# Two sparse graph-attention layers on one Trainium2 core: a distance mask for owners, fewer small copies in the first phase, and an earlier write of the second table

## The chip, the cores and the metric

The kernel runs on one core of one Trainium2 chip. The metric is device time in microseconds: the median of 3 timed runs before the change is 1710.78 us (1709.91 to 1712.45). The profile is one further execution of 1709.7 us, of which the traced span is 1708.0 us.

## The reference

Both layers work on 8192 nodes with 128 features. The adjacency matrix is dense int32, 8192 x 8192 (268 MB), but holds only about nine ones in a row.

```python
h = jnp.maximum(_layernorm(x, axis=-1), 0.0)
x = x + _L0_gnn_ref(h, adj, W, a)
h = jnp.maximum(_layernorm(x, axis=-1), 0.0)
x = x + _L1_gnn_ref(h, adj, Wq, bq, Wk, bk, Wv, bv)

# layer 0                                    # layer 1
h = x @ W                                    q, k, v = x @ Wq.T + bq, x @ Wk.T + bk, x @ Wv.T + bv
e = leaky_relu(s1[:, None] + s2[None, :])    scores = q @ k.T / sqrt(d)
scores = where(adj > 0, e, -9e15)            scores = where(adj > 0, scores, -9e15)
attention = softmax(scores, axis=1)          attention = softmax(scores, axis=-1)
out = elu(attention @ h)                     out = elu(attention @ v)
```

## The kernel before, in words

Work goes by tiles of 128 rows, 64 of them, each phase in groups of four. The first phase (the functions called `survey`, one on each engine) reads the adjacency matrix once, turns each row into a list of at most 24 neighbours, and does layer 0. The second phase (`attend`) uses the kept lists and does layer 1; it does not read the matrix again.

One step `t` of the first phase works on several tiles at once:

- SyncE (SP) loads the matrix in quarters of a tile (128 x 2048 int32, 1 MB, line 455) into two tile buffers. A load waits until ScalarE has turned the quarter that lay there into a mask (`mask_done`). In the same in-order queue stand the load of a tile's own rows of the first table (line 468), and once in four steps the write of four finished tiles to the second table (line 489).
- ScalarE (ACT) makes the mask of four quarters (line 1186), copies what TensorE dealt (line 1238), takes the exponentials (lines 1213, 1217) and the two halves of elu (1208, 1209), and writes four normalised tiles into `stage` (line 1257), from which the second table is written. Before it may overwrite `stage` it waits for the last write (`table1_in`).
- TensorE (PE) packs the mask into numbers (line 1384); VectorE (DVE) takes the largest ones (706), decodes and sorts them into a list (726 to 768).
- A row has six regular slots; rows with more neighbours get their others from "owners". `count` and `split` work out from a running sum where each row's owned entries begin and end; `mark` builds the 0/1 matrix `mine` (128 x 384) of who owns which entry (lines 795 and 798); TensorE deals the entries by it (1445); `pick` (815 to 839) makes the nine indices of a row's gathers.
- GpSimd (POOL) issues nine indirect gathers a tile from the first table (line 579), three steps before DVE uses them in `score0` (852), `maxima` (859 to 863), `weigh` (873), `add_slot` (880) and `total` (889).

The lags are fixed by hand: `PICK, LATE, DONE = 3, 6, 7` steps behind the extraction. Each engine runs its list in the written order; semaphores join them. SP's loop body for the writes reads, before the change: at the first step of a group (`b == 0`) wait for `stage_done`, `(g - 3) * GROUP`, and write group `g - 4`. ACT fills `stage` for group `g - 3` at the ends of the first two steps of group `g`.

## Time and profile before

| what | value |
|---|---|
| median of 3 runs | 1710.78 us |
| the profiled execution | 1709.7 us |
| its span | 1708.0 us |
| PE, DVE, ACT, POOL busy | 68%, 72%, 51%, 67% of the span |
| bytes moved | 372.42 MB, mean 218 GB/s |
| first phase (table of first rows to last write of the second table) | to about 957 us |
| second phase | about 957 to 1708 us |

The busy shares are means over two phases with different limits. In the first half of the span the DMA engines are full and carry 370 to 400 GB/s; in the second half they carry some 60 GB/s. A wait row names who released the waiting instruction, which need not be the cause further back.

### The profile page before, as it was taken

Reading aid. Unit: us, or ns where it says so; the run is one execution under the profiler, and the core shown is the slowest. Engines: PE = TensorE matmul, PEld = TensorE weight load, DVE = VectorE, ACT = ScalarE, POOL = GpSimd, SP = SyncE. Lnnn points to the kernel's source line nnn. Section 1 sums busy time; section 2 is a strip of 40 time slices with the busy share of each in tenths; the row PEclk is TensorE's granted clock in tenths of the full one; section 3 lists DMA queues with packets and bytes.
Section 4 is the critical chain, followed back from the end, with each engine's and each line's share of the span. In section 5 each row is a group of like instructions: output and inputs, shape, how many; then the busy total and the mean of one; then the engine's idle time right before and its main releaser. Section 6 shows DMA issues by size and latency. Waiting matters only on the chain.

```text
span 1708.0 us, 23183 instructions
## 1 busy us (share of the span) xinstructions
PE 1161.2 (68%) x5314; PEld 919.1 (54%) x5362; DVE 1235.4 (72%) x6788; ACT 875.2 (51%) x1763; POOL 1137.7 (67%) x1206
## 2 busy tenths in 40 slices
PE   2667775776777777667765567766766677677765
PEld 1344553554544454455444467655666666666664
DVE  3567996998888898888897366656665665665665
ACT  2768876777777778777752222333233233322322
POOL 1237775766666766667667477777777777777773
PEclk9878877777777777777765555666666666666655
DMA  9879999999999999999932122222222222222221
GB/s 294 344 256 386 395 395 399 396 397 374 371 389 382 390 381 381 387 377 381 392 82 62 48 59 58 65 64 65 64 66 65 65 64 64 65 65 63 65 65 41
DMA packets 122264, 372.42 MB, mean 218 GB/s; under 512 B 34577, under 2 KB 67858, under 8 KB 89362
## 3 DMA queue, kind: packets, MB, share of 16 engines
q1 hardware_dynamic: 75458, 289.83, 44.2%
q0 software_dynamic: 38464, 81.08, 17.0%
q10 hardware_dynamic: 8208, 0.03, 0.3%
q8 instruction: 46, 0.75, 0.2%
q14 instruction: 88, 0.72, 0.1%
HBM read 358.12 MB, written 12.72 MB: 217 GB/s over the span
## 4 chain that ended last, share of the span: by engine, by line
POOL 34%; DVE 20%; DMA 15%; issue 13%; PE 10%; ACT 6%; SPq 2%; POOLq 0%; ACTq 0%; DVEq 0%
POOL arena L609 32%; DMA table<-arena 13%; ACT arena L1186 4%; PE psum L1445 4%; PE psum L1431 3%; POOL arena L579 2%; DMA arena<-in_adj_dram 1%; DVE arena L765 1%; DVE arena L798 1%; DVE arena L873 1%; DVE arena L768 1%; DVE arena L880 1%; PE psum L1417 1%; DVE arena L889 1%; SPq L452 1%
## 5 line engine op out<-in xcount | busy, mean ns | idle before, releaser
L579 POOL DMA_INDIRECT arena<-table,arena x576 | 556.1, 966 | 263.8 <-issue 159.6
L609 POOL DMA_INDIRECT arena<-table,arena x576 | 553.2, 960 | 184.1 <-issue 175.0
L1186 ACT ACTIVATE arena<-arena 128x2048 bf16<-128x2048 int32 x256 | 485.0, 1895 | 32.7 <-DMA arena<-in_adj_dram 32.7
L1384 PE MATMUL psum<-arena 128*128 128x512 bf16 x976 | 281.6, 433 | 26.3 <-ACT arena L1186 22.3
L880 DVE SCALAR_TENSOR_TENSOR arena<-arena 128x131 f32<-128x131 f32 (+1 forms) x768 | 268.2, 349 | 15.5
L1431 PE MATMUL psum<-arena 128*128 128x131 f32 (+1 forms) x768 | 201.4, 434 | 104.1 <-ACT arena L1319 102.4
L1417 PE MATMUL psum<-arena 128*128 128x18 f32 x768 | 135.4, 308 | 174.5 <-DVE arena L846 174.5
L1431 PEld LDWEIGHTS psum<-arena 128*128 128x128 f32 x768 | 180.6, 331 | 107.8 <-issue 107.8
L1417 PEld LDWEIGHTS psum<-arena 128*128 128x128 f32 x768 | 129.4, 249 | 191.9 <-DVE arena L846 191.6
L1127 DVE CUSTOM_DVE_ANT_0 arena<-arena,psum 128x129 f32<-128x129 f32 x192 | 45.2, 286 | 229.7 <-DMA arena<-table,arena 229.7
L1424 PE MATMUL psum<-arena 128*128 128x1 f32 x768 | 135.7, 292 | 103.0 <-DVE arena L863 101.9
L1424 PEld LDWEIGHTS psum<-arena 128*128 128x128 f32 x768 | 136.1, 253 | 126.6 <-DVE arena L863 116.9
L1384 PEld LDWEIGHTS psum<-arena 128*128 128x128 bf16 x1024 | 113.8, 117 | 159.0 <-issue 71.8
L1213 ACT ACTIVATE arena<-arena 128x7 f32<-128x7 f32 x128 | 38.4, 300 | 278.1 <-DVE arena L863 278.1
L1445 PE MATMUL psum<-arena 128*128 128x155 f32 x384 | 116.2, 471 | 69.5 <-DVE arena L798 69.3
L1340 ACT ACTIVATE arena<-psum 128x384 f32<-128x384 f32 x64 | 31.5, 493 | 236.6 <-PE psum L1551 236.6
L1445 PEld LDWEIGHTS psum<-arena 128*128 128x128 f32 x384 | 91.8, 308 | 74.3 <-DVE arena L798 74.0
L1550 PE MATMUL psum<-arena 128*128 128x128 f32 x384 | 119.3, 413 | 1.0 <-DVE arena L1119 1.0
L1551 PE MATMUL psum<-arena 128*128 128x129 f32 x384 | 116.6, 403 | 0.0
L706 DVE MAX8 arena<-psum 128x8 f32<-128x64 f32 x512 | 105.2, 222 | 0.1
L1550 PEld LDWEIGHTS psum<-arena 128*128 128x128 f32 x384 | 103.8, 330 | 1.5 <-issue 1.5
L1133 DVE CUSTOM_DVE_ANT_0 arena<-arena 128x129 f32<-128x129 f32 x448 | 101.4, 291 | 0.0
(204 smaller groups left out, 1989.9 us busy)
## 6 DMA issues: line engine op xcount, KB each, us to landing
arena<-in_adj_dram SPq DMA_DIRECT2D x256, 1024.0 KB, 15.3
arena<-table,arena POOLq DMA_INDIRECT x1152
table<-arena POOLq DMA_DIRECT2D x32, 132.0 KB, 5.2
arena<-table SPq DMA_DIRECT2D x64, 66.0 KB, 13.3
table<-arena SPq DMA_DIRECT2D x16, 256.0 KB, 15.3
arena<-table SPq DMA_DIRECT2D x64, 64.0 KB, 1.9
out_dram<-arena SPq DMA_DIRECT2D x16, 256.0 KB, 2.4
arena<-in_x_dram SPq DMA_DIRECT2D x4, 0.5 KB, 12.1
```

What stands on the lines that cost most here:

```text
L579: pool.indirect_dma_start(Gt[:, v % GROUP, c + 1, :], None, table0, bass.IndirectOffsetOnAxis(idx_now[:, v % GROUP, c:c + 1], 0))\
L609: pool.indirect_dma_start(Gt[:, t % GROUP, c + 1, 0:D], None, table1, bass.IndirectOffsetOnAxis(idx_now[:, t % GROUP, c:c + 1], 0))\
L706: ins = nc.vector.max(words[:, b // 2, b % 2, 8 * n:8 * n + 8], V[b % 2][:, PLACE * n:PLACE * (n + 1)])
L880: nc.vector.scalar_tensor_tensor(out=acc_sb[:, k, 0:width], in0=Gt[:, r, c, 0:width], scalar=p10[:, k, c:c + 1], in1=acc_sb[:, k, 0:width] ...
L1186: nc.scalar.activation(mask[:, k, q * QUARTER:(q + 1) * QUARTER], adj_sb[:, k, q, :], ACT.Relu, accum_out=sum_all[:, bass.ds(tile, 1), q:q ...
L1384: nc.tensor.matmul(V[k], shifted[:, s, :], mask[:, k, s * 512:(s + 1) * 512], start=(s == 0), stop=False)
L1417: last = nc.tensor.matmul(by_slot_ps[k], owned[:, r, c, :], slot_e[:, k, c, :], start=(c == 0), stop=(c == CHUNKS - 1))
L1424: last = nc.tensor.matmul(max_ps[k][:, c:c + 1], mine[:, r, c * P:(c + 1) * P], neg_max[:, k, :], start=True, stop=True)
L1431: last = nc.tensor.matmul(acc_ps[k][:, 0:width], weighted[:, c, :], Gt[:, r, OWN + c, 0:width], start=(c == 0), stop=(c == CHUNKS - 1))
L1445: last = nc.tensor.matmul(deal_ps[v % 2][:, c, :], mine[:, v % GROUP, c * P:(c + 1) * P], dealt[:, v % GROUP, :], start=True, stop=True)
L1550: nc.tensor.matmul(own_ps[m][:, c, :], mine_c, ident[:, :], start=True, stop=True)
L1551: last = nc.tensor.matmul(uq_ps[m][:, c, :], mine_c, u_row[:, j, P:], start=True, stop=True)
```

## The change

The mask of owners is computed from a distance: an entry at place `j` belongs to a row if `|2j + 1 - (start + end)| < end - start`. ScalarE computes the absolute value (`measure_spans`, which the second phase already used), and VectorE compares it with the length in one instruction in place of two. `count` and `split` keep the length and the negated sum for it (`len_all`, `mid_all`). In `pick` the copies of the half scores and one of the two padding computations go, and all nine indices are clamped by one instruction, for which the three owned ones are first put behind the six regular ones in `dealt`. `score0` adds the half scores in two parts, from where they lie. `maxima` reads the padding from `pad_all` (bf16) in both phases; the second phase loses its copy of it and its three preparing instructions. SP writes the second table at the third step of a group (`b == 2`), for group `g - 3`, in place of the first step of the next group.

```diff
-                    if b == 0 and (not isinstance(g, int) or 0 <= g - 4 < G):
-                        sp.wait_ge(stage_done, (g - 3) * GROUP)
+                    if b == 2 and (not isinstance(g, int) or 0 <= g - 3 < G):
+                        sp.wait_ge(stage_done, (g - 2) * GROUP)
...
+                nc.vector.tensor_scalar(len_all[:, at], count_all[:, at], -float(REGULAR), 0.0, ALU.add, ALU.max)\
+                  .then_inc(count_done, 1)
...
-                nc.vector.tensor_tensor(pre_all[:, at], ends_ps, over16[:, :], ALU.subtract).then_inc(split_done, 1)
+                nc.vector.scalar_tensor_tensor(out=mid_all[:, at], in0=ends_ps, scalar=-2.0, in1=over16[:, :],
+                                               op0=ALU.mult, op1=ALU.add).then_inc(split_done, 1)
...
-            def mark(v, b, pair):
-                dve.wait_ge(split_done, 3 * (pair + 1))
-                nc.vector.tensor_scalar(from_end[:, :], iota16[:, :], end_all[:, bass.ds(v, 1)], None, ALU.is_ge)\
-                  .then_inc(fe_done, 1)
-                dve.wait_ge(fe_done, v + 1)
-                nc.vector.scalar_tensor_tensor(out=mine[:, b, :], in0=iota16[:, :],
-                                               scalar=dealt[:, b, LISTED + SLOTS:LISTED + SLOTS + 1], in1=from_end[:, :],
-                                               op0=ALU.is_ge, op1=ALU.subtract).then_inc(mine_done, 1)
+            def mark(v, b):
+                dve.wait_ge(dist_done, v + 1)
+                nc.vector.tensor_scalar(mine[:, b, :], dist[:, b % 2, :], len_all[:, v:v + 1], None, ALU.is_lt)\
+                  .then_inc(mine_done, 1)
...
-                nc.vector.tensor_copy(s1_10[:, b, OWN:ROWS], ps[:, :, DEALT - 1]).then_inc(pick_done, 1)
+                nc.vector.tensor_scalar(pad_all[:, at, :], one(dealt[:, b, P:LISTED + SLOTS]), 0.0, NEG, ALU.is_le, ALU.mult)\
+                  .then_inc(pick_done, 1)
...
-                nc.vector.tensor_scalar(idx_now[:, b, 0:REGULAR], dealt[:, b, LISTED:over], 0.0, float(N), ALU.max, ALU.min)\
-                  .then_inc(pick_done, 1)
...
-                nc.vector.tensor_scalar(s1_10[:, b, 0:OWN], ones[:, 0:OWN], dealt[:, b, DEALT - 1:DEALT], None, ALU.mult)\
-                  .then_inc(pick_done, 1)
+                after(4)
+                nc.vector.tensor_reduce(dealt[:, b, over:over + CHUNKS], picked[:, :, :], AX.X, ALU.add).then_inc(pick_done, 1)
                 after(5)
-                nc.vector.tensor_reduce(node_q[:, :], picked[:, :, :], AX.X, ALU.add).then_inc(pick_done, 1)
-                nc.vector.tensor_scalar(pad[:, b, :], dealt[:, b, P:LISTED + SLOTS], 0.0, NEG, ALU.is_le, ALU.mult)\
-                  .then_inc(pick_done, 1)
-                after(7)
-                nc.vector.tensor_scalar(idx_now[:, b, REGULAR:], node_q[:, :], 0.0, float(N), ALU.max, ALU.min)\
+                nc.vector.tensor_scalar(idx_now[:, b, :], dealt[:, b, LISTED:over + CHUNKS], 0.0, float(N), ALU.max, ALU.min)\
                   .then_inc(idx_done, 1)
...
-                nc.vector.tensor_tensor(e10[:, :], Gt[:, r, :, D], s1_10[:, r, :], ALU.add).then_inc(e_done, 1)
+                nc.vector.tensor_scalar(e10[:, 0:OWN], Gt[:, r, 0:OWN, D], self_s1[:, u, 1:2], None, ALU.add).then_inc(e_done, 1)
+                nc.vector.tensor_tensor(e10[:, OWN:ROWS], Gt[:, r, OWN:ROWS, D], owned_list[:, r, :, DEALT - 1], ALU.add)\
+                  .then_inc(e_done, 1)
...
+            def measure_spans(t):
+                nc.scalar.activation(dist[:, t % 2, :], iota_odd[:, :], ACT.Abs, bias=mid_all[:, t:t + 1]).then_inc(dist_done, 1)
...
+                    if live(t, PICK):
+                        act.wait_ge(split_done, 3 * (v // 2 + 1))
+                        at_least(act, mine_done, v - 1)
+                        measure_spans(v)
```

On VectorE, `pick` of one tile in the steady part before the change (815 is the entries' places, 819 the one-hot, 825 and 830 pick the owned index, 834 clamps it, 839 keeps the nine):

```order
L815 TENSOR_TENSOR arena<-arena 128x3 [waits owned_done]
L817 COPY arena<-arena 128x3
L819 TENSOR_TENSOR arena<-arena 128x54 [waits pick_done]
L822 TENSOR_SCALAR arena<-arena 128x6
L825 TENSOR_TENSOR arena<-arena 128x54 [waits pick_done]
L827 TENSOR_SCALAR arena<-arena 128x7
L830 TENSOR_REDUCE arena<-arena 128x3 [waits pick_done]
L831 TENSOR_SCALAR arena<-arena 128x25
L834 TENSOR_SCALAR arena<-arena 128x3 [waits pick_done]
L836 TENSOR_SCALAR arena<-arena 128x25
L839 COPY arena<-arena 128x9 [waits idx_done]
```

and after it (806 the places, 808 the padding, 811 the one-hot, 815 and 818 the owned index, 820 the clamp of nine):

```order
L806 TENSOR_TENSOR arena<-arena 128x3 [waits owned_done]
L808 TENSOR_SCALAR arena<-arena 128x25
L811 TENSOR_TENSOR arena<-arena 128x54 [waits pick_done]
L815 TENSOR_TENSOR arena<-arena 128x54 [waits pick_done]
L818 TENSOR_REDUCE arena<-arena 128x3 [waits pick_done]
L820 TENSOR_SCALAR arena<-arena 128x9 [waits pick_done]
L823 COPY arena<-arena 128x9 [waits idx_done]
```

Eleven instructions became seven. Before, every instruction that waits for the one it needs had an independent one in front of it; now the last five follow each other directly.

On VectorE, `weigh` and `mark` before (873 weighs the owner matrix, 795 and 798 are `mark`, 883 begins the chain of seven rows):

```order
L846 TENSOR_TENSOR arena<-arena 128x54 [waits score_done]
L873 TENSOR_TENSOR arena<-arena 128x384 [waits owned_done,p_done]
L795 TENSOR_SCALAR arena<-arena 128x384 [waits split_done]
L798 SCALAR_TENSOR_TENSOR arena<-arena 128x384 [waits fe_done]
L883 TENSOR_SCALAR arena<-arena 128x131
```

and after (859 weighs, 790 is `mark`, 869 begins the chain):

```order
L840 SCALAR_TENSOR_TENSOR arena<-arena 128x10 [waits e_done]
L830 TENSOR_TENSOR arena<-arena 128x54 [waits score_done]
L859 TENSOR_TENSOR arena<-arena 128x384 [waits owned_done,p_done]
L790 TENSOR_SCALAR arena<-arena 128x384 [waits dist_done]
L869 TENSOR_SCALAR arena<-arena 128x131
```

`mark` is one instruction, and it now waits for ScalarE (`dist_done`), where it used to wait for VectorE's own `split`.

On ScalarE, the start of a step after the change (1200 is the exponential of the owners' gap, 1178 the distance, 1166 a quarter's mask, 1225 the copy of the dealt entries; without 1178 the rows are those of before):

```order
L1166 ACTIVATE arena<-arena 128x2048 [waits adj_in10,packed]
L1200 ACTIVATE arena<-arena 128x3 [waits gap_done]
L1178 ACTIVATE arena<-arena 128x384 [waits mine_done,split_done]
L1166 ACTIVATE arena<-arena 128x2048 [waits adj_in11]
L1166 ACTIVATE arena<-arena 128x2048 [waits adj_in12]
L1225 ACTIVATE arena<-psum 128x465 [waits deal_done]
```

One instruction has come in, behind the exponential and ahead of three others of the step.

On SyncE, the last groups of the first phase, written out after its loop. Before (455 a quarter of the matrix, 468 a tile's own rows, 489 the write of the second table):

```order
L455 DMA arena<-in_adj_dram 128x2048 x4
L468 DMA arena<-table 128x132
L489 DMA table<-arena 128x4x128
L455 DMA arena<-in_adj_dram 128x2048 x4
L468 DMA arena<-table 128x132 x4
L489 DMA table<-arena 128x4x128
L468 DMA arena<-table 128x132 x3
L489 DMA table<-arena 128x4x128 x3
```

and after (447, 460 and 481 in the same roles):

```order
L447 DMA arena<-in_adj_dram 128x2048 x4
L460 DMA arena<-table 128x132
L447 DMA arena<-in_adj_dram 128x2048 x4
L460 DMA arena<-table 128x132 x2
L481 DMA table<-arena 128x4x128
L460 DMA arena<-table 128x132 x4
L481 DMA table<-arena 128x4x128
L460 DMA arena<-table 128x132
L481 DMA table<-arena 128x4x128 x2
```

The write stands two steps later in a group, for a group of tiles one younger, so a given group's write stands two steps earlier than before.

## Rows read from the trace of the kernel before

**Rows 1.** The page: the span in 40 slices of 42.7 us.
```profile
DVE  3567996998888898888897366656665665665665
DMA  9879999999999999999932122222222222222221
GB/s 294 344 256 386 395 395 399 396 397 374 371 389 382 390 381 381 387 377 381 392 82 62 48 59 58 65 64 65 64 66 65 65 64 64 65 65 63 65 65 41
```

**Rows 2.** Busy time by stretch: PE, PEld, DVE, ACT, POOL, granted clock, DMA share, GB/s.
```profile
160.00:300.00 140.00, 96.54 (x444) 65.90 (x451) 120.30 (x650) 101.46 (x149) 96.70 (x102) 0.77 1.02 397
300.00:860.00 560.00, 404.79 (x1812) 279.68 (x1845) 494.97 (x2668) 424.61 (x629) 380.36 (x395) 0.76 1.00 382
...
960.00:1700.00 740.00, 517.21 (x2424) 472.43 (x2424) 449.18 (x2614) 218.44 (x759) 551.47 (x575) 0.62 0.24 63
...
646.00:652.00 6.00, 2.27 (x11) 2.18 (x12) 3.35 (x14) 6.00 (x8) 4.48 (x6) 0.67 0.97 343
610.00:640.00 30.00, 23.32 (x102) 16.48 (x105) 28.25 (x150) 22.95 (x34) 21.93 (x23) 0.74 1.02 399
```

**Rows 3.** Waits in 300 to 860 us: in total, times, longest, us.
```profile
ACT arena L1257 <- DMA table<-arena: 39.4, 11, 4.9
ACT arena L1217 <- DVE arena L867: 35.6, 33, 1.8
DVE arena L873 <- ACT arena L1217: 34.7, 11, 4.1
```

**Rows 4.** ScalarE's timeline in one group: start, us, instruction, idle before it.
```profile
646.00 0.88 ACT L1257 ACTIVATE arena<-arena 128x128 f32<-128x128 f32 x2 [2.95 <-DMA table<-arena]
...
648.67 0.19 ACT L1217 ACTIVATE arena<-arena 128x3 f32<-128x3 f32 x1
```

**Rows 5.** SyncE's timeline, the same group.
```profile
630.97 0.41 SPq L489 DMA_DIRECT2D table<-arena  x1
```

**Rows 6.** Line 489 alone, the whole span.
```profile
DMA to landing us min/median/max: 2.3/15.3/23.4
```

**Rows 7.** DMA in 300 to 860 us: packets and bytes; issues, KB each, us to landing.
```profile
DMA packets 49648, 214.17 MB, mean 382 GB/s; under 512 B 9938, under 2 KB 21194, under 8 KB 27480
...
arena<-in_adj_dram SPq DMA_DIRECT2D x171, 1024.0 KB, 15.3
```

**Rows 8.** VectorE's timeline, one tile: `pick`, then `mark`.
```profile
631.34 0.15 DVE L815 TENSOR_TENSOR arena<-arena 128x3 f32<-128x3 f32 x1
...
631.52 0.22 DVE L819 TENSOR_TENSOR arena<-arena 128x54 f32<-128x54 f32 x1
...
631.77 0.22 DVE L825 TENSOR_TENSOR arena<-arena 128x54 f32<-128x54 f32 x1
...
632.56 0.29 DVE L898 SCALAR_TENSOR_TENSOR arena<-arena 128x128 f32<-128x128 f32 x1
...
634.65 0.16 DVE L852 TENSOR_TENSOR arena<-arena 128x10 f32<-128x10 f32 x1
...
635.65 0.31 DVE L795 TENSOR_SCALAR arena<-arena 128x384 f16<-128x384 f16 x1
...
636.54 0.30 DVE L883 TENSOR_SCALAR arena<-arena 128x131 f32<-128x131 f32 x1
```

**Rows 9.** The second phase's owner mask on VectorE, by its line.
```profile
L1114 DVE TENSOR_SCALAR arena<-arena x64: 410/414/589, 957.1 to 1672.1; 128x384 f32<-128x384 f16 x64
```

**Rows 10.** The distance on ScalarE, by its line.
```profile
L1312 ACT ACTIVATE arena<-arena x64: 597/599/615, 956.5 to 1652.5; 128x384 f16<-128x384 f16 x64
```

**Rows 11.** The last quarters' masks on ScalarE: min/median/max ns, first and last start.
```profile
L1186 ACT ACTIVATE arena<-arena x8: 1892/1894/1896, 853.6 to 874.1; 128x2048 bf16<-128x2048 int32 x8
```

**Rows 12.** GpSimd's timeline: the first gather of the last four tiles, and the last.
```profile
890.88 0.95 POOL L579 DMA_INDIRECT arena<-table,arena  x1 [1.02 <-DVE arena L834]
...
935.89 0.95 POOL L579 DMA_INDIRECT arena<-table,arena  x1 [0.30 <-issue]
```

**Rows 13.** The DMA rate at the end of the matrix, 825 to 875 us in 40 slices.
```profile
GB/s 389 385 408 346 255 404 402 409 385 401 392 398 392 387 403 400 417 388 415 385 411 399 388 400 299 205 88 74 74 137 71 23 0 0 0 54 54 54 54 108
```

60 lines of the change are left out of this document (21 added, 39 removed).

## The prediction

> **What bounds the kernel now.** I read the page's slices first. Up to about 850 us the DMA engines are full and VectorE is near nine tenths; after it DMA carries some 60 GB/s and no engine stands out [rows 1]. The two phases need separate answers. The second takes 740 us of the windows table, in which GpSimd issues 575 gathers, 1.29 us each with its gaps, 551 us of them busy, while VectorE is busy 449 us and ScalarE 218 us [rows 2]: GpSimd's issuing bounds it, and nothing of the change touches GpSimd. So only the first phase can give time.
>
> There I compared stretches by bytes. From 160 to 300 us DMA moves 397 GB/s at a share of 1.02; from 300 to 860 us it moves 382 [rows 2]. The difference is not spread evenly: 610 to 640 us has 399 GB/s, the six microseconds from 646 have 343 with VectorE busy only 3.35 of 6 [rows 2]. The waits say what happens there. Eleven times, once a group of four tiles, ScalarE's copy into `stage` (1257) waits for the write of the second table, 39.4 us together, and as often VectorE's `weigh` (873) waits for ScalarE's exponential 1217, 34.7 us together [rows 3]. In the timeline these are one event: ScalarE idles 2.95 us, starts 1257 at 646.00, has a quarter's mask behind it, and gives VectorE its exponential at 648.67 [rows 4]. The write it waited for was issued at 630.97 [rows 5] and such a write takes 15.3 us to land, behind the matrix quarters in the same queue [rows 6]: it is needed one step after it is issued. While ScalarE stands, it frees no quarter, SP issues no load, and the flow thins. A load takes 15.3 us to land [rows 7], at 382 GB/s 5.8 MB in flight of 8.4 MB of buffers; the reserve is two quarters, and a stall uses it up.
>
> VectorE carries 495 us of 560 and 34.7 us of waits [rows 2, 3], so between stalls it is the other near-bound: per tile 51.5/4 = 12.9 us, of which 0.8 us is that wait.
>
> **The change part by part.** *The write of the table.* It is now issued at about the third step of a group and needed at the end of the first step of the next, some 36 us later (three steps less a little), against a slowest landing of 23.4 us [rows 6]. The stall goes, also the large one at 276 us, which lies where DMA is full anyhow. On SP the write now stands in front of the quarter loads of the fourth step. Its new wait is for `stage`, which ScalarE fills just before the mask that the next load needs, so nothing queued behind it is held longer. The row loads (468) behind it have two steps to spare.
>
> *The mask.* Before: 795 starts at 635.65 and the chain of rows at 636.54, 0.89 us for both [rows 8]. After: one instruction of the form of 1114, 0.414 us long [rows 9]; instructions that don't wait start some 0.08 us before the last one ends, so about 0.33 us. It gives 0.55 us a tile. New on ScalarE: 0.60 us a tile [rows 10], about 0.5 in sequence. ScalarE is busy 425 of 560 us [rows 2], 9.8 us of a tile's 12.9, and waits 35.6 us for VectorE at 1217 alone [rows 3]; 10.3 fits. What is queued behind it are two masks and the copy of the dealt entries. VectorE reaches `mark` 1.0 us after 852 [rows 8], and `weigh` in front of it lies parallel to the distance, so I take no wait for it. The bounds: 0 and 0.6 us a tile, and I take 0, since `weigh` did not wait in the steps without the stall (11 waits in all, one a group [rows 3]).
>
> *`pick`.* Before: 815 to 898 (the next work after it), 1.22 us for eleven instructions [rows 8]. Counting seven out of eleven as a gain would be wrong: 819 starts at 631.52 and takes 0.22, and 825, which needs it, starts at 631.77 [rows 8]; an instruction that needs the one before it can't start before its end, and the four that go lay in such gaps. Now places to one-hot 0.18, one-hot to pick 0.25, to sum 0.25, to clamp 0.23, to copy 0.20, and 0.08 for the copy, 1.19 us. Gain nothing, with bounds of -0.1 and +0.3 us. `score0` adds one instruction, 0.07 us, `count` one per two tiles; `maxima` reads other bytes at the same size. VectorE's sum is 0.45 us a tile less, 29 us over 64 tiles if VectorE were alone.
>
> *The second phase* loses a small copy a tile and three instructions at its start, all beside GpSimd's gathers: 0, at most 1 us.
>
> *What is late next.* Without stalls and with 0.45 us less, VectorE needs 12.9 - 0.8 - 0.45 = 11.6 us a tile. GpSimd needs nine gathers at 1.29 = 11.6. The DMA engines need, per tile, 4.19 MB of matrix, 0.61 MB of gathered rows (9 x 128 x 528 B), 0.07 MB of own rows and 0.07 MB of table write, 4.93 MB; at 397 GB/s 12.4 us. So DMA takes over and three quarters of VectorE's gain are lost under it. The write's new place changes no byte of this.
>
> *The sum.* The matrix ends now at about 855.5 us, where the rate falls [rows 13]. Of the 214.2 MB from 300 us on [rows 7] about 213.7 are moved by then; at 397 GB/s they take 538 us, with one more tile's gathers (0.6 MB) 540: the matrix ends at 840, 15.5 us earlier. Behind it lies a second gain. Now the last mask starts at 874.1 and ends at 876.0 [rows 11], 20.5 us after the last byte, because the stalled engines work off two stored tiles. With DMA as the bound nothing is stored: the last mask follows its quarter, 1.9 us of work and some 2 for what stands before it on ScalarE, at 844. Everything behind the last mask keeps its length. From there GpSimd sets the pace: the last four tiles' gathers start at 890.88 and the last at 935.89 [rows 12], 35 intervals of 1.29 us, in which GpSimd waits for VectorE only about 1 us twice. So the whole end moves by 876 - 844 = 32 us. 1709.7 - 32 = 1677.7 for a profiled execution; the median of before lies 1.1 above its profile, so 1679.
>
> The Trainium skill, page "DMA: Bandwidth & Descriptors", section "Where 436 GB/s comes from", gives 435 GB/s as the ceiling of the memory ports and about 358 GB/s as the limit of HBM for a core. This trace does not agree with the second, since it holds 397 GB/s for 140 us [rows 2]. By the first a tile would take 11.3 us, DMA would not take over, and the second rival below would be the case.
>
> **The rivals.** *The backlog stays.* The stalls go and the matrix ends 15.5 us earlier, but masks, extraction and picks still end 20 us behind it, because their mutual waits hold that distance: 1695. For it speaks the 15.3 us landing in the steady part [rows 7], against it that VectorE is faster than the stream by 0.8 us a tile and would close 20 us in 25 tiles.
>
> *DMA is not the bound.* The rate rises with demand. VectorE and GpSimd at 11.6 us a tile from 300 us on give 1.25 us for each of some 45 tiles, 56 us: 1654. Against it: the rate is 397 and 399 GB/s in stretches of different demand, at a share of 1.02 [rows 2].
>
> *No change.* The stall moves to another wait of the same group, or the write still lands late: 1710. Against it is the margin of 36 us over 23.4.
>
> *Slower.* ScalarE is late with the distance. If a mask is running when VectorE releases 1217, the exponential comes up to 1.9 us late, then the distance 0.6, and VectorE, which has only some 1.3 us of other work before `mark`, stands up to 1.5 us in each tile. For 64 tiles that is 96 us, against 3.4 us x 11 + 29 = 66 us of gain on VectorE, and the time would be 1740. It decides from a mean of 1.0 us a tile. Against it: 1217 was waiting for VectorE in 33 steps [rows 3], so mostly ScalarE is there first.
>
> **How the numbers follow.** Forecast 0.68, backlog stays 0.12, DMA not the bound 0.08, no change 0.06, slower 0.06. For the forecast's own range I take 395 to 400 GB/s (3 us either way), the last mask 1 to 6 us later than said, and the bounds of `pick`: 1672 to 1686. The range that should hold eight of ten takes in the backlog and part of the way to the second rival: 1666 to 1697. Faster by more than 0.2% (3.4 us, about what a measurement of this kernel tells from no change): the first three, 0.88. Within it 0.06, slower 0.06.
>
> **What would show it.** Right: no wait of the `stage` copy for the table; a DMA rate of 395 to 400 GB/s from 160 us to the matrix's end, which comes at 838 to 843; ScalarE's masks now waiting for the matrix, and its last one ending within 6 us of the last byte; landing times of the loads at 20 us or more; VectorE busy some 0.45 us a tile less and idle more than a microsecond; the last gather of the first table near 904; a second phase of unchanged length. Wrong: dips in the rate once a group as before; `mark` waiting for the distance; the rate steady but the last mask 15 us or more behind it (then 1695); or a rate above 405 GB/s.

## The result and the profile after

The changed kernel takes 1695.73 us (median of 4 runs, 1692.4 to 1699.37), the kernel before beside it 1710.35 (4 runs): a ratio of 0.9915, 95% interval 0.9903 to 0.9927. It is faster, by 14.6 us where 31.8 were forecast. The profiled execution took 1699.37 us, the slowest of the four; its span is 1697.6 us (before: 1708.0), so the profiled pair shows 10.4 us of the gain.

The page's slices after, one step of 42.4 us each:
```profile
DVE  3567988888888888888887366656655665566655
DMA  9869999999999999999942122222222222222221
GB/s 292 345 225 391 397 398 399 400 401 396 390 386 394 365 371 390 382 394 371 386 125 61 51 59 57 65 64 66 64 66 64 66 64 64 66 64 64 66 66 39
```
Against [rows 1]: from 170 to 382 us the rate is 397 to 401, before 395 to 399. From 384 us on it was 371 to 392 before; now that comes a slice or two later (390, 386, 394, then 365 to 394). The busy times by stretch, columns as in [rows 2]:
```profile
160.00:300.00 140.00, 105.51 (x480) 70.92 (x479) 122.79 (x649) 112.82 (x172) 104.89 (x108) 0.77 1.02 398
300.00:860.00 560.00, 423.46 (x1843) 281.80 (x1842) 477.83 (x2523) 443.75 (x673) 378.45 (x391) 0.77 1.01 385
960.00:1700.00 740.00, 520.25 (x2408) 474.32 (x2406) 442.91 (x2550) 218.26 (x761) 542.72 (x568) 0.61 0.25 62
```
385 GB/s over the long stretch against 382, and 397 in the forecast. The waits in 300 to 860 us, in total, times, longest:
```profile
ACT arena L1166 <- DMA arena<-in_adj_dram: 115.1, 123, 2.6
...
DVE arena L859 <- ACT arena L1200: 24.8, 31, 1.8
...
DVE arena L783 <- PE psum L1453: 19.5, 17, 2.1
```
The `stage` copy no longer waits for the table [rows 3]; in its place ScalarE's mask (1166) waits for the matrix 123 times. The loads land after 22.7 us in place of 15.3 [rows 7]:
```profile
DMA packets 50172, 215.43 MB, mean 385 GB/s; under 512 B 9971, under 2 KB 21592, under 8 KB 27867
...
arena<-in_adj_dram SPq DMA_DIRECT2D x172, 1024.0 KB, 22.7
```
VectorE's timeline answers to [rows 8]: `mark` (790) holds its slot for 0.33 us, and `pick` runs from 806 to the next work, 884:
```profile
628.91 0.42 DVE L790 TENSOR_SCALAR arena<-arena 128x384 f32<-128x384 f16 x1
629.24 0.28 DVE L869 TENSOR_SCALAR arena<-arena 128x131 f32<-128x131 f32 x1
...
635.76 0.16 DVE L806 TENSOR_TENSOR arena<-arena 128x3 f32<-128x3 f32 x1
...
636.99 0.29 DVE L884 SCALAR_TENSOR_TENSOR arena<-arena 128x128 f32<-128x128 f32 x1
```
The end of the matrix, 825 to 875 us in 40 slices of 1.25 us, against [rows 13], and ScalarE's last three masks:
```profile
GB/s 358 424 401 406 395 385 411 415 369 395 411 408 395 372 383 408 418 379 413 388 408 408 382 389 332 155 67 123 173 77 74 80 87 116 80 54 44 71 54 54
```
```profile
861.61 1.91 ACT L1166 ACTIVATE arena<-arena 128x2048 bf16<-128x2048 int32 x1
864.49 1.91 ACT L1166 ACTIVATE arena<-arena 128x2048 bf16<-128x2048 int32 x1 [0.88 <-DMA arena<-in_adj_dram]
867.61 1.90 ACT L1166 ACTIVATE arena<-arena 128x2048 bf16<-128x2048 int32 x1
```
The bulk still ends at 856.5 us (before 855.5). What follows it is odd: for some ten more microseconds 67 to 173 GB/s are moved, where the gathers alone take 54 at the row's end, and a mask that starts at 864.49 still waits for the matrix. The last mask starts 6.5 us earlier than before [rows 11]. The gathers of the first phase (571) and of the second (601), nanoseconds of one, first and last start, and line 609 of the kernel before, the second phase's:
```profile
L571 POOL DMA_INDIRECT arena<-table,arena x576: 938/944/1333, 128.3 to 927.9; - x192
L601 POOL DMA_INDIRECT arena<-table,arena x576: 940/944/1072, 950.2 to 1674.7; - x192
```
```profile
L609 POOL DMA_INDIRECT arena<-table,arena x576: 943/947/1154, 958.0 to 1685.6; - x192
```
The first phase's last gather comes 8.0 us earlier (935.89 in [rows 12]), and the second phase is 3.1 us shorter from first to last gather, 724.5 against 727.6. These 11.1 us are the profiled pair's gain of 10.4; the stretches between the two phases and behind the last gather are 0.7 us longer.

**What a landing shows.** For each DMA the trace holds sixteen landing events, one for each DMA engine's part; a load is complete with the last. The "landing" of the views is only that last one. I took the 256 matrix loads and worked out how long the sixteenth part comes behind the fifteenth, as the median over the loads of 50 us (some 15 of them). A landing event does not say which engine it is of. The table, in us, has the kernel before and after and seven of the experiments told below; its last two columns are the fifteenth and sixteenth landing of the very last load.

| kernel | 200 | 300 | 400 | 500 | 600 | 800 | last load |
|---|---|---|---|---|---|---|---|
| before | 0.6 | 3.0 | 7.0 | 4.4 | 5.9 | 6.0 | 858.5, 864.4 |
| after | 0.2 | 4.4 | 8.3 | 9.5 | 10.0 | 9.0 | 858.4, 867.3 |
| e1, new write, rest old | 1.1 | 5.3 | 9.7 | 9.4 | 9.2 | 9.5 | 860.7, 869.5 |
| e2, old write, rest new | 1.4 | 5.0 | 6.8 | 5.5 | 6.2 | 6.4 | 858.4, 864.6 |
| e3, write by ScalarE | 0.9 | 5.4 | 9.3 | 12.4 | 15.0 | 14.5 | 851.0, 864.9 |
| e4, no write in the matrix | 0.1 | 4.7 | 8.8 | 11.7 | 14.6 | 15.5 | 842.4, 857.2 |
| e5, e4 without gathers | 0.6 | 0.4 | 0.6 | 0.6 | 0.4 | | 788.2, 788.5 |
| e13, blocks for gathers | 0.8 | 4.6 | 8.3 | 10.7 | 12.7 | 12.5 | 809.5, 821.8 |
| e16, own rows 120 + 8 | 1.2 | 5.6 | 9.0 | 13.0 | 15.5 | 14.6 | 855.5, 870.0 |

One part of sixteen falls behind, from 200 to 400 us by 2.0 us in each 50 us (2.2 in e4), and in the kernel before as well, by 1.6. That is what the tail above is: one engine, a sixteenth of 400 GB/s or 25, works off what it is behind. All of a load's users wait for it. When it is 10 to 15 us behind, three to five loads of 3.1 us each (a quarter of the tile's 12.4), the other engines have done all that is queued, and the bulk rate comes down to its pace.

So the profile says where the forecast's time is: the last load lands at 867.3 us in place of 864.4. For the late engine ("the slow one" below) the change gained nothing. What it gained is behind it: the last mask began 9.7 us after the last landing and now begins 0.3 us after it.

### The profile page after: what moved, and what is told of

Same layout as the page of the kernel before. It is cut to its first block, busy times and chain, and to the rows that moved or that the text cites. A ratio compares the mean times of both kernels' runs of the same rounds, so it can differ in the third digit from the quotient of the medians.

```text
span 1697.6 us, 23065 instructions
## 1 busy us (share of the span) xinstructions
PE 1189.3 (70%) x5362; PEld 930.2 (55%) x5362; DVE 1201.7 (71%) x6497; ACT 904.9 (53%) x1827; POOL 1137.3 (67%) x1206
## 4 chain that ended last, share of the span: by engine, by line
DMA 40%; POOL 33%; issue 13%; ACT 5%; DVE 4%; PE 3%; SPq 2%; POOLq 0%; ACTq 0%; DVEq 0%
DMA arena<-in_adj_dram 37%; POOL arena L601 32%; ACT arena L1166 4%; DMA table<-arena 1%; POOL arena L571 1%; SPq L444 1%; DMA arena<-table 1%; DVE arena L658 1%; SPq L447 1%; PE psum L1368 0%; DVE arena L866 0%; PE psum L1429 0%; DMA arena<-table,arena 0%; PE psum L1393 0%; PE psum L1415 0%
## 5 line engine op out<-in xcount | busy, mean ns | idle before, releaser
L1368 PE MATMUL psum<-arena 128*128 128x512 bf16 x1024 | 301.6, 437 | 71.7 <-ACT arena L1166 71.3
L1401 PE MATMUL psum<-arena 128*128 128x18 f32 x768 | 144.6, 321 | 143.7 <-DVE arena L830 143.2
L1415 PEld LDWEIGHTS psum<-arena 128*128 128x128 f32 x768 | 179.9, 330 | 107.7 <-issue 107.7
L1401 PEld LDWEIGHTS psum<-arena 128*128 128x128 f32 x768 | 138.5, 265 | 161.9 <-DVE arena L830 161.8
L1408 PEld LDWEIGHTS psum<-arena 128*128 128x128 f32 x768 | 138.1, 257 | 117.2 <-DVE arena L849 108.4
L1429 PEld LDWEIGHTS psum<-arena 128*128 128x128 f32 x384 | 94.8, 317 | 31.9 <-DVE arena L790 31.4
L1534 PEld LDWEIGHTS psum<-arena 128*128 128x128 f32 x384 | 103.7, 329 | 1.5 <-issue 1.5
## 6 DMA issues: line engine op xcount, KB each, us to landing
arena<-in_x_dram SPq DMA_DIRECT2D x4, 0.5 KB, 12.1
```

What stands on the lines that cost most here:

```text
L1368: nc.tensor.matmul(V[k], shifted[:, s, :], mask[:, k, s * 512:(s + 1) * 512], start=(s == 0), stop=False)
L1401: last = nc.tensor.matmul(by_slot_ps[k], owned[:, r, c, :], slot_e[:, k, c, :], start=(c == 0), stop=(c == CHUNKS - 1))
L1408: last = nc.tensor.matmul(max_ps[k][:, c:c + 1], mine[:, r, c * P:(c + 1) * P], neg_max[:, k, :], start=True, stop=True)
L1415: last = nc.tensor.matmul(acc_ps[k][:, 0:width], weighted[:, c, :], Gt[:, r, OWN + c, 0:width], start=(c == 0), stop=(c == CHUNKS - 1))
L1429: last = nc.tensor.matmul(deal_ps[v % 2][:, c, :], mine[:, v % GROUP, c * P:(c + 1) * P], dealt[:, v % GROUP, :], start=True, stop=True)
L1534: nc.tensor.matmul(own_ps[m][:, c, :], mine_c, ident[:, :], start=True, stop=True)
```

## The experiments

**The two halves apart (e1, e2).** e1 is the kernel before with only the write's place changed:
```
-  if b == 0 and (... 0 <= g - 4 < G):  sp.wait_ge(stage_done, (g - 3) * GROUP)
+  if b == 2 and (... 0 <= g - 3 < G):  sp.wait_ge(stage_done, (g - 2) * GROUP)
```
e2 is the changed kernel with this edit undone.

> The kernel before with only the write of the second table moved to the third step of a group. The changed kernel's matrix ended at the same time as before (about 856 us), and its queue of loads was full. Theory A (the stream of DMA work has its own length; the stall was covered by it, and only the backlog behind the matrix is won): the wait for the table goes, the matrix ends at 855 to 858 us, the time falls by 8 to 12 us, to about 1700, less than the whole change because VectorE is slower in closing the backlog. Theory B (the new place of the write blocks the loads' queue on SyncE and this took the place of the stall): the same blocking is seen here, load issues of 5 us or more once a group. If neither, and the gain came from VectorE's lighter step: no change from 1710.

> The changed kernel with the write back at the first step of a group. Theory A: the stalls return, each costs VectorE about 3.5 us a group, and its lighter step (0.45 us a tile) wins 1.8 us a group of it back: matrix end at about 856, time 1702 to 1708. Theory B: without the write in front of a full queue no load issue above 3 us in the steady part, and the rate is that of before. Were the lighter step the source of the whole gain, the time would be 1696.

e1: 1702.32 us, ratio 0.9948 (0.9931 to 0.9964). e2: 1702.74 us, 0.9961 (0.9947 to 0.9975). Each brings about half; 7.9 and 7.5 us against 14.6 for both, within their intervals a plain sum. The waits in 300 to 860 us of e1 and of e2:
```profile
ACT arena L1186 <- DMA arena<-in_adj_dram: 132.6, 130, 2.4
```
```profile
ACT arena L1244 <- DMA table<-arena: 46.5, 11, 5.9
...
DVE arena L859 <- ACT arena L1200: 42.2, 11, 5.7
```
In e1 the stall is gone and DMA is the bound without any of the lighter VectorE work. Its last load even lands at 869.5 us, 5 us later than before; the gain is again the backlog behind it, and the last gather of the first phase comes at 931.4 us in place of 935.9. In e2 the stall is back, and a part of VectorE's saving is spent waiting at it (42.2 us against 34.7). Of e2's gain only 3.0 us are the first phase's (last gather at 932.9); 3.3 are the second phase's, 724.3 us from first to last gather against 727.6.

**The write's own cost (e3, e4).** e3 issues the write by ScalarE in place of SyncE. e4 issues none while the matrix streams: the copies into `stage` come after step 62, into the matrix's buffers, which are free by then.
```
- stage = place([GROUP, D])
+ stage = adj_sb.rearrange("p k q c -> p (k q c)").bitcast(F32)[:, 0:T * D].rearrange("p (t d) -> p t d", t=T)
+ LATE_STAGE = {63 + n: (2 * n, 2 * n + 1) for n in range(7)}   # then 70: (14,), 72: (15,)
```

> The changed kernel with the table's write issued by ScalarE, directly behind its own copies into stage, in its own queue. Theory B: no SyncE load is issued behind a write, the 5 to 8 us issues go, the rate stays at 397 GB/s, the matrix ends at about 842 and the time is about 1682. Theory A: the same bytes and rows pass the same 16 engines, the rate falls once a group as before, matrix end 854 to 858, time 1694 to 1698; ScalarE's own issue may be blocked instead.

> The changed kernel with no write of the second table while the matrix is read: the normalised rows of groups 0 to 13 are made in steps 63 to 69 into the matrix buffers, which are free by then, and written from there. Theory A in the form that the writes themselves thin the stream: 397 GB/s through to the end, matrix end at about 840 to 843, time 1680 to 1684. If the dips come from the gathers or from anything else in the stream: matrix end 853 to 857 (3.4 MB less is 8 us at most), time about 1690 to 1696. Theory B predicts the gain here too, by the queue: 1682.

e3: 1694.12 us, 0.9904 (0.9887 to 0.992), not told apart from the changed kernel. e4: 1690.16 us, 0.9885 (0.9868 to 0.9901), the fastest kernel with the whole computation of which more than one run was taken. What e3 is about shows in SyncE's timeline of the changed kernel, then that of e4 at the same time (a row of x4 has the issues of four loads, from the first's start to the last's end):
```profile
600.67 0.41 SPq L481 DMA_DIRECT2D table<-arena  x1
602.65 16.15 SPq L447 DMA_DIRECT2D arena<-in_adj_dram  x4
...
619.93 4.61 SPq L447 DMA_DIRECT2D arena<-in_adj_dram  x4
```
```profile
608.54 9.46 SPq L450 DMA_DIRECT2D arena<-in_adj_dram  x4
```
Behind the write the four loads take 16 us to go out, and the next four come in a bunch; e1 has the same (16.45 us for its four at 602.04 us). With the write in another queue (e3) the other fifteen engines finish 7.4 us sooner (851.0), but the slow one only 2.4 us (864.9), and the time stays. In e4 the write's packets are gone as well, and the slow engine is done 10.1 us sooner, at 857.2. The windows of e4, 160 to 300, 300 to 450 and 500 to 800 us:
```profile
160.00:300.00 140.00, 105.30 (x475) 71.38 (x482) 123.35 (x654) 110.60 (x163) 105.62 (x109) 0.78 1.02 397
300.00:450.00 150.00, 113.06 (x500) 77.42 (x509) 131.13 (x689) 116.98 (x174) 102.14 (x107) 0.77 1.02 399
500.00:800.00 300.00, 226.90 (x984) 151.19 (x1000) 256.75 (x1363) 231.94 (x342) 203.61 (x212) 0.77 1.01 386
```
Even with no write the rate falls from 399 to 386. That left the question of the following runs.

**The gathers (e5, e13).** Both are e4 without the first phase's gathers; the neighbours' rows are then not gathered, and the output is another. e5 sets the rows to zero, e13 has SyncE load as many bytes in blocks:
```
+ sp.dma_start(Gt[:, k, 1:ROWS, :].rearrange("p c d -> p (c d)"),
+              table0[1:1 + P * (ROWS - 1), :].rearrange("(p c) d -> p (c d)", p=P)).then_inc(rows_set[k], 16)
```

> The kernel without table writes during the matrix, with the first phase's row gathers left out too (the rows are set to zero, so the output is not the reference's). In the parent the transfers run at 399 to 400 GB/s until about 450 us and at 383 to 390 from 500 us on, although eight loads are always outstanding, and the last masks still wait for their loads 10 us after the bulk rate has fallen at 841 us. Theory 'one DMA engine lags': one of the sixteen engines has some 4% more to do per tile than the others, all loads need all sixteen, so the others run ahead until the eight outstanding loads are used up and then go at that engine's pace. If the extra work is not the gathers, the late rate of matrix bytes stays 4% below the early one here too, and the last masks again come 8 to 12 us after the bulk has ended; matrix bytes per tile are then 4.26 MB and the end comes near 790 to 805 us. Theory 'the gathers' own packets are slow late in the stream': without them there is no late fall, rate near 400 GB/s from 200 us to the end, and the last mask within 4 us of the bulk's end. No third reading of the gathers' bytes alone (0.66 MB a tile, 13%) explains a change with time.

> The kernel without table writes and without the first phase's gathers, with one more load a tile by SyncE in their place: 128 pieces of 4752 bytes, always the same table rows (0.61 MB a tile as the gathers', near their packet size of 4224 bytes; the neighbours' data is then not the reference's). Matrix tiles then take 4.93 MB each as in the parent and the queue stays full. If the gathers make one engine lag: the sixteenth landing stays within 1 to 2 us of the fifteenth to the end, and the rate is level near 399 GB/s from 300 to 800 us, with the matrix ending near 830 us. If the cause is there without gathers (instruction fetches or the engine itself): the sixteenth landing falls behind by about 1 us in each 25 us up to some 10 us, and the rate steps down from 399 to 383 to 388 between 450 and 550 us, as in the parent.

e5: 1634.72 us (one run, before 1709.09). It doesn't decide. With 0.61 MB a tile less, DMA isn't the bound (the mask waits for the matrix 26.2 us in all, 24.8 of them once at the start), the rate is 369 GB/s from 300 to 450 us, so even an engine 4% slower keeps up, and the lag is nil. e13: 1653.97 us (one run, before 1711.02) puts the load back, and with it the lag. Its windows, and the tail from 780 to 830 us:
```profile
160.00:300.00 140.00, 106.72 (x492) 71.98 (x501) 126.48 (x689) 116.10 (x169) 0.00 (x0) 0.78 1.02 417
...
500.00:800.00 300.00, 228.97 (x1029) 156.56 (x1049) 264.89 (x1439) 242.70 (x361) 0.00 (x0) 0.78 1.01 404
```
```profile
GB/s 433 382 389 333 375 406 426 413 439 413 433 303 299 416 422 423 419 419 419 419 419 406 317 155 298 205 26 26 26 26 26 26 26 86 259 247 30 0 7 0
```
Here the one engine is plain to see: with nothing else running, 26 GB/s for 9 us, a sixteenth of 417. The slow engine is there without a single gather; the theory that gathers make it slow has fallen. The Trainium skill, page "DMA: Bandwidth & Descriptors", section "Latency and other measured facts", notes that two of the sixteen engines are usually slower and guesses at the descriptor rings of GpSimd's DMAs as the cause; e13 has no such DMA in this stretch, so the guess doesn't explain the late engine here. The levels say besides that the same bytes run at 417 GB/s in blocks and at 397 as gathered rows.

**Code fetches (e6, e7, e9, e10).** The queues called instruction move code. e6 adds 128 waits a tile that are already met on SyncE, e7 64 on TensorE, e9 48 on GpSimd, e10 32 on ScalarE, all to e4:
```
+ for _ in range(64):
+     pe.wait_ge(pool_consts, 15)
```

> As the parent without table writes, with 32 waits that are already met put behind each matrix load on SyncE (128 more instructions a tile, computation unchanged). Theory 'one DMA engine lags because it also carries the engines' code' : more code means more bytes in the queues called instruction, on an engine that carries code. If it is the lagging one its extra work rises, the fall of the rate starts earlier than 450 us and ends lower, some 365 to 372 GB/s from 500 us on in place of 383, and the matrix ends near 860 to 875 us in place of 841. If SyncE's code goes by another engine than the lagging one, or the lag has nothing to do with code, the rate is as in the parent within 3 GB/s. Theory 'gathers slow late': as in the parent in either case.

> As the parent without table writes, with 64 waits that are already met put into each tile on TensorE (64 more instructions a tile, computation unchanged). Theory 'one DMA engine lags because it also carries the engines' code': one of the two instruction queues moves some 2 times the packets, and if that queue is the lagging engine's the rate from 500 us on is 373 to 379 GB/s in place of 383 and the matrix ends near 850 us in place of 841. If TensorE's code goes by another engine, as in the parent within 3 GB/s. Theory 'gathers slow late': as in the parent.

> As the kernel without table writes during the matrix, with 48 waits that are already met put ahead of each first-phase tile's gathers on GpSimd (computation unchanged). In the parent one of a load's sixteen landings falls behind the other fifteen by about 1.1 us more in each two tiles (25 us) from 250 us on, until it is 10 us late at 475 us and the rate falls from 399 to 383 GB/s. Theory 'the lagging DMA engine also carries the instruction queues' (some 1.06 us for each packet of the one and 0.33 us for each of the other, together 10.4 us between 248 and 476 us): 48 more instructions a tile are more bytes in one of those queues. If both queues are the same engine's, the lag grows faster, is 10 us before 430 us, and the late rate is 377 to 380 GB/s. If GpSimd's code is another engine's, a second engine falls behind beside the first. Theory 'gathers make it lag': the gathers are the same, no change: 10 us at 475 us, 383 GB/s.

> As the kernel without table writes during the matrix, with 32 waits that are already met put into each tile on ScalarE (computation unchanged). Theory 'the lagging DMA engine also carries the instruction queues': as for GpSimd's code, with 32 in place of 48: the last landing is 10 us late some 30 us earlier than in the parent (475 us) and the late rate 379 to 381 GB/s, or, if ScalarE's code is another engine's, a second engine lags beside the first. Theory 'gathers make it lag': no change.

One run each: 1689.47, 1707.10, 1687.66 and 1687.83 us (before 1709.09 for the first two, 1708.86 for the others); but for e7 that is e4's 1690, as far as one run tells. The instruction queues in 300 to 800 us, of e4, e7 and e9:
```profile
q8 instruction: 14, 0.23, 0.2%
q14 instruction: 27, 0.22, 0.1%
```
```profile
q8 instruction: 18, 0.29, 0.2%
q14 instruction: 26, 0.21, 0.1%
```
```profile
q8 instruction: 14, 0.23, 0.2%
q14 instruction: 34, 0.28, 0.1%
```
TensorE's code comes by q8, GpSimd's by q14 (and so does ScalarE's: 32 packets in e10). More of q14 leaves the late rate at 387 to 388 and the slow part's distance from the median landing at 12 to 13 us in 450 to 500 us (12.1 in e4); but the fifteenth part is then 3.6 us behind the median against 1.8. So GpSimd's and ScalarE's code loads a second engine, not the slow one. In e6 the count did not rise past the unrolled start (27), since SyncE's code is a loop there; up to 300 us q14 has 16 packets from 150 us on against 10 in e4, and the fifteenth part is 4.3 us behind the median in 250 to 300 us (2.7 in e4), so SyncE's code loads a second engine as well. e7 failed as a test: with its waits DMA was no longer the bound (the mask waits for the matrix only 26.6 us, nearly all at the start), and the lag was 3.0 us at 500 and 0.4 at 800.

**One engine's share (e8, e12, e14, e15, e16).** e8 adds to e4 one row of 3 KB behind each load. e12 and e14 load the fourth quarter of each tile in two pieces, e15 does so with e13's blocks and e16 with e4's own rows:
```
+ for lo, hi in ((0, 120), (120, P)):        # e14: ((0, 112), (112, P))
+     sp.dma_start(adj_sb[lo:hi, k, q, :], adj[bass.ds(tile * P + lo, hi - lo), q * QUARTER:]).then_inc(adj_in[k][q], 16)
```

> As the parent without table writes, with one more load of a single row of 3 KB behind each matrix load (4 a tile, 12 KB a tile, into a buffer that nothing reads). Averaged over sixteen engines that is 0.2% of a tile's bytes and would cost 1 us in all. Theory 'one DMA engine lags': a row of 3 KB is one engine's work, some 0.13 us each, 0.5 us a tile or 4% of that engine's time. If it falls on the lagging engine the late rate goes to about 368 to 372 GB/s and the fall starts earlier; if it always falls on another single engine, that one lags as far as the first and the rate stays near 383; if it goes round all sixteen, no change. Theory 'gathers slow late': no change.

> As the kernel without table writes during the matrix, with the fourth quarter of each matrix tile loaded as 120 rows and 8 rows (same bytes, same destination, one more DMA a tile). If the engines get rows in equal blocks, 120 rows leave one engine without its 8 and 8 rows go to one or to eight engines, so shares change by 1 to 8 rows of a tile's 32 per engine, 3 to 25%. Theory 'one engine lags for want of time': the lag must change: it vanishes and the late rate stays near 397 (matrix end 830 to 836 us, time 1684 to 1687 us) if the relieved engine is the lagging one; another or the same engine lags sooner and the rate is 370 or lower (time over 1695 us) if an engine gets more. Theory 'the late fall has nothing to do with shares': 383 GB/s late and 1690 us as before. If rows are cut and dealt evenly whatever the shape, the same.

> As the kernel without table writes during the matrix, with the fourth quarter of each tile loaded as 112 rows and 16 rows: equal shares of 7 and 1 rows for each of sixteen engines, but another engine for most rows than in the loads of 128. If unequal shares made the loads of 120 and 8 rows slow (253 GB/s): here nothing changes, 383 to 399 GB/s and a time of 1688 to 1692 us. If it was that two engines write the same rows' memory at once, the packets of 8 KB are slower here too (499 ns there, 329 ns in the parent) and the rate is 260 to 350 GB/s, the time 1750 to 2000 us.

> As the kernel with rows in blocks (no gathers, no table writes; 0.61 MB a tile of blocks in their place, the data then not the reference's), with the block load of each tile made as 120 and 8 pieces in place of 128. If 120 pieces go to fifteen engines, eight each, and the 8 to eight others, one each, seven engines get 8 pieces a tile as before, eight get 9, and one gets none: it is spared 8 pieces of 4752 B, about 1.6 us a tile, three times the 0.5 us a tile that the slow engine loses. If the slow engine is the spared one, the sixteenth landing no longer falls behind by 12 us and the late rate does not step down by 3% from the early one. If it is another: the lag grows as in the parent or faster, 2.1 us in 50 us and more, and the step is there. Rival, that rows of another division collide with the matrix's in memory: the rate is below 417 GB/s from the start, without a step in time.

> The whole computation, no table writes during the matrix, with each tile's own rows (66 KB) loaded as 120 and 8 rows. One engine is spared 8 pieces of 528 B, some 0.2 us a tile of the 0.5 us a tile that the slow engine loses. If the slow engine is the spared one, the sixteenth landing falls behind by 1.2 to 1.5 us in 50 us in place of 2.1, the last load lands some 6 to 10 us earlier than the parent's 857 us and the time is 1681 to 1686 us against the parent's 1690. If it is one of the eight that get a ninth row: 0.03 us a tile more, 1690 to 1692. If the shifted rows collide with the matrix's: slower, 1695 or more.

e8: 1692.73 us (one run). A second part now comes late: in 450 to 500 us the fifteenth is 12.0 us behind the median (1.8 in e4) and the sixteenth 2.0 behind it, 14.0 in all against 12.1; the rate in 500 to 800 us is the same 386. So 12 KB a tile on one engine, 0.2% of the bytes, make that engine as late as the slow one, and it is not the slow one. A little extra work on one engine is thus enough for the whole effect. The Trainium skill, page "DMA: Bandwidth & Descriptors", section "Why a DMA increments its semaphore by 16 and not by 1", says that a transfer of one row takes the lowest-numbered engine; by that the slow engine is another than the first, and the landings agree.

e12: 2026.16 us; e14: 1940.07; e15: 1844.37 (one run each). All three are far slower, e14 with equal shares too. The queue of the loads, bytes in MB and share of 16 engines in 300 to 860 us, of e4, e12 and e14:
```profile
q1 hardware_dynamic: 31628, 185.12, 84.0%
```
```profile
q1 hardware_dynamic: 21582, 126.71, 84.7%
```
```profile
q1 hardware_dynamic: 24988, 144.52, 82.5%
```
A share of 84.0% of 16 engines for 560 us and 185.12 MB is 40.7 us of an engine for each MB; in e12 it is 59.9, in e14 51.1. The engines are as busy and each packet is slower. So the collapse is not from shares: each of e14's two pieces has sixteen landings, so its shares are even. It would fit that rows go by another engine than in the loads of 128, and two engines write into one part of the memory. The Trainium skill, page "DMA: Bandwidth & Descriptors", section "The descriptor swizzle", has each engine of a 128-row transfer writing through one port; that another division of the rows breaks this is my inference. These runs show the slower packets, not the port.

e16, six runs: 1705.18 us, ratio 0.9967 (0.9955 to 0.998), against e4's 0.9885: 120 + 8 costs 15 us even on 66 KB a tile. Its lag grows by 7.8 us from 200 to 400 us, by 8.7 in e4, where 4.8 to 6 were expected from a relief, so the engine spared by 120 rows is not the slow one, or the collisions hid the relief. e15's lag (9 to 11 us from 400 to 700 us) doesn't decide either, with its packets slowed.

**A check without gathers at small packets (e11).** e5 with nine more loads of the own rows for each tile.

> The kernel without table writes and without the first phase's gathers, with nine more loads of the tile's own rows by SyncE in their place (the same bytes per tile, 0.66 MB in packets of one row; each node's neighbours are then the node itself, so the output is not the reference's). Unlike the run without gathers the DMA engines stay the bound, since they have the same bytes to move in smaller packets. Theory 'instruction queues': no gather is left, yet one landing of sixteen falls behind by some 4% of the time that passes while the queue is full, to about 10 us, and the rate then steps down by 3 to 4% of its early value. Theory 'gathers make it lag': the last landing stays within 1 to 2 us of the one before it to the end, and the rate is level from 200 us on.

1704.51 us (one run). The windows:
```profile
160.00:300.00 140.00, 102.88 (x462) 69.94 (x462) 118.40 (x635) 106.31 (x158) 0.00 (x0) 0.76 1.02 387
...
500.00:800.00 300.00, 219.53 (x978) 148.48 (x978) 246.08 (x1334) 222.87 (x332) 0.00 (x0) 0.76 1.01 372
```
The step of 4% is there, the lag is 2 to 3 us and not 10. A mixed answer: with nine small loads more for each tile in the queue the others stop at a smaller lag, and why was not followed; e13 is the cleaner form of this test.

## Why the prediction was wrong

The direction was right, and so was what bounds the kernel after the change; the size was not. By the prediction's steps:

- *The stall goes.* Right: 39.4 us of waits [rows 3] are none, and e1 shows that this alone gives 8 us.
- *The mask, `pick`, VectorE.* Right but for small sizes: `mark`'s slot is 0.33 us, `pick` takes 1.23 us (1.22 before, 1.19 forecast), and VectorE is busy 477.8 us of 560 against 495.0 [rows 2], 0.4 us for each of some 43 tiles (0.45 forecast). `mark` doesn't wait for the distance; the rival "slower" has no sign in the waits.
- *DMA is late next.* Right: ScalarE waits for the matrix 123 times, and loads land after 22.7 us.
- *At 397 GB/s to the end.* **The step that failed.** The sum took the rate of 160 to 300 us [rows 2] for the stream's steady rate and blamed the fall behind it on the stall. The stall had its part in the dips, but the fall is there with no stall (e1, 383 GB/s from 500 to 800 us) and with no write at all (e4, 386). In 160 to 300 us the slow engine was not yet so far behind that the others ran out of loads. It gets through the loads about 4% more slowly (2.0 us in 50), 397 x 0.96 = 381, near the 382 that the kernel before showed in [rows 2]; the prediction put what one engine has to do besides the loads at nothing. The stall hardly cost this engine time before the change either: it had work stored, 4.4 us and more behind the fifteenth in the median of every 50 us from 350 us on, and its last part landed at 864.4 against 867.3. All bytes moved from 300 us to the last landing, over that time, say the same: 380.3 GB/s before, 381.1 after, and 379.3, 382.7, 383.6 and 381.4 in e1 to e4, with and without the stall, the write's block and the write. The stalls emptied the other fifteen. So the matrix's end was forecast 15.5 us earlier and came 1 us later.
- *The last mask within 4 us of the last byte.* Right by its mechanism, wrong by its place. The mask does follow its quarter, 0.3 us behind the landing. But the 20.5 us between the fall of the rate [rows 13] and the last mask's end [rows 11] were taken for backlog of the engines; only 9.7 us of them were, 8.9 were the slow engine's tail. The tail is there after the change, 10.8 us. The row that would have warned stands in [rows 13]: 74, 74, 137, 71, 23 GB/s behind the fall.
- *Everything behind keeps its length.* Nearly: the last gather is 60.3 us behind the last mask's start, before 61.8 [rows 11, 12].
- *The second phase.* Forecast 0, at most 1 us. It is 3.1 us shorter; the page's mean of an indirect DMA is 955 ns in place of 960, and 576 of them make 2.9 us. From first to last gather the sixteen traces with the new second phase have 723.3 to 724.6 us, and the two with the old one 727.6 (before) and 726.0 (e1). So it comes from the lighter second phase, at 1.4 us at least, and the 1.6 us between the two old ones say how well a single trace knows it.

The rival "backlog stays" named 1695 us, and the time is 1695.7, but it is not what happened: it had the matrix ending at 840 and the backlog kept, where the matrix did not move and the backlog went. Its number is right by chance.

## What to carry to other kernels

A load is done when the last of sixteen engines is, and work that falls on one of them alone, a code fetch (e13) or a short row (e8), can make every load late. Before a stream's best rate is put into a sum as what it could do throughout, look at what one engine does: in the rate behind the stream's end a rest of a sixteenth of the full rate, or loads that are still waited for after the rate has fallen, say that one engine sets the pace, and that emptying a stall will feed only the others. Bytes taken out of the stream do help then (e4: 10 us), and here transfers of other than a full set of rows cost far more than any balance they could bring (e16, 15 us).

## What was not expected of the hardware

- One DMA engine gets through a full queue about 4% more slowly than the others, with and without gathers, and falls behind from some 200 us on. In e13 it is the engine of q14's fetches of 8 KB: every 25 us a fetch of 0.33 us and behind it a load packet of 0.96 us in place of 0.31. It is not the engine that a one-row load takes (e8), nor the one of GpSimd's and ScalarE's code (e9, e10).
- q14's fetches do not all go by one engine.
- The same bytes at 417 GB/s (e13) or 397 (e4), the one with blocks of 4752 B by SyncE, the other with rows gathered by GpSimd.
- A table write of 512 rows of 512 B holds up SyncE's next load issues, 16.15 us for four where they take 9.46 without it.
- Loads split as 112 + 16 or 120 + 8 rows in one quarter of four take the rate from 386 to 305 and 255 GB/s (500 to 800 us).
